# A message-passing layer on one core: edge tiles of 121 edges in blocks of 24, gathered into a ring of 192 tiles

## Chip, cores and metric

The kernel runs on one core of one Trainium2 chip. The metric is the device time in microseconds (us) of one execution; lower is better. All arithmetic is float32.

## What is computed

There are 12,500 nodes with 128 features, and 400,000 edges, each with a source, a destination and 64 attributes. The destinations are sorted. Cut to what matters:

```python
h = maximum(layernorm(x), 0)
m = relu(concat([h[src], edge_attr]) @ msg_w1 + msg_b1) @ msg_w2 + msg_b2
agg = segment_sum(m, dst, num_segments=12500)
u = relu(concat([h, agg]) @ upd_w1 + upd_b1)
out = x + u @ upd_w2 + upd_b2
```

## The kernel before, in words

**Node stage.** 25 groups of 500 nodes (NP = 125 partitions by ROWS = 4). VectorE takes the row statistics, ScalarE normalises, TensorE turns each group and multiplies it with the source part of the message weights. The product plus bias, `table`, is a 12,500 by 128 array in DRAM, stored by `store_table` on SP's queue (L295). TensorE also forms `update`, the node part of the update layer, which stays in SBUF transposed. Meanwhile GpSimd (POOL) gathers raw rows of `x` for the first 75 edge tiles (`early`, L368), because the table doesn't exist yet.

**Edge stage.** 3,200 tiles of EDGES = 125 edges, five tiles (TILES) to a chunk, so 640 chunks. One gather is one indirect DMA on POOL's queue: it fetches 125 rows of 512 bytes into one tile, one row in each partition (L380). Before its five gathers a chunk waits for its indices (L281 loads them on SP's queue after VectorE is done with the chunk that had the slot). The ring `rows` holds five chunks, 25 tiles. Per chunk:

- TensorE multiplies the attributes with their weights (L433, five matmuls with 64 rows of contraction, 128 columns each), one chunk ahead;
- VectorE adds the gathered rows into `hidden` (`sum_rows`, L785), ScalarE applies the relu (L613);
- VectorE builds a 0/1 mask of 5 by WINDOW = 128 columns (`make_masks`, L826), which says which node of a window of 128 nodes each edge goes to, and adds the five masks up (`sum_masks`, L834);
- TensorE sums the hidden rows of the chunk by node (`hidden_sums`, L467, five matmuls into one PSUM region), VectorE copies this out (`copy_sums`, L841), TensorE multiplies it with the joined weights (`update_sums`, L476, L477), and VectorE adds the result to 128 columns of `update` at the chunk's base (`accumulate`, L849).

The first 15 chunks used are the "early" ones (EARLY = 15): their rows are normalised, turned and multiplied on the spot (L443 to L454), one of them among ten others in each of the 15 rounds of the first loop. The engines have fixed orders of work, written out in loops over five slots; semaphores tie them together. A branch (`dve.If(span < WINDOW)`) takes a slow path if any chunk spans 128 nodes or more.

**Final stage.** When all edges are added, ScalarE takes the relu of `update` (L649), TensorE multiplies by the last weights (L542), VectorE adds to `x_all` (L946), which has stayed in SBUF since the start with the bias added during the edge stage (L910), and SP stores it (L343).

## Time and profile before

| | |
|---|---|
| median of 3 runs | 4913.87 us (4913.0 to 4914.27) |
| the profiled execution | 4917.07 us |
| its span in the trace | 4915.3 us |
| mean granted TensorE clock, of full speed | 0.608 |
| busy: PE, DVE, ACT, POOL | 71%, 46%, 12%, 79% |
| gathers | 75 of `x`, 3,125 of `table` |

The span runs from the first to the last recorded instruction. "Busy" of POOL's gather is the time that the record of the instruction covers; "idle before" is the gap ahead of it, and "issue" means that the gap waited for nothing that the profile shows. A queue's name ends in q (SPq). Rows of the trace are quoted in a section of their own below.

### The profile page before, as it was taken

The page shows a single profiled execution, that of the slowest core. Times are in us where ns is not written, and L with a number is a line of the kernel's source. Part 1 is how long each engine was busy: PE and PEld are TensorE (multiplying, and loading weights), DVE is VectorE, ACT ScalarE, POOL GpSimd, SP SyncE. Part 2 cuts the span into 40 slices and gives each one's busy share as a digit, 9 for nine tenths or more (in the row PEclk, how much of TensorE's full clock was granted, in tenths as well). Part 3 has the DMA queues.
Part 4 walks back from the last instruction along what each step waited for, and adds up shares of the span by engine and source line. Part 5 has one row for each costly group of instructions (what it writes and reads, how often), then busy time and mean ns, then how long its engine had stood idle before and what let it go on. Part 6 is the DMA issues. An engine that isn't in the chain of part 4 may idle for free.

```text
span 4915.3 us, 59369 instructions
## 1 busy us (share of the span) xinstructions
PE 3511.1 (71%) x16139; PEld 3183.0 (65%) x16139; DVE 2248.7 (46%) x3651; ACT 595.7 (12%) x887; POOL 3881.7 (79%) x3208
## 2 busy tenths in 40 slices
PE   5677777777677767766777677767776677767766
PEld 3666666666666666666666666666666666666666
DVE  5455555555444444444444444444444444444444
ACT  5111111111100000001010001000100010001002
POOL 7777777777778787877777777777777777777774
PEclk8666666666655555556555655655565655565566
DMA  7322222222222222222222222222222222222223
GB/s 174 73 67 64 69 66 67 68 66 67 64 64 64 65 65 64 64 64 64 64 66 64 64 64 65 64 64 64 65 65 64 64 64 66 64 64 64 65 64 87
DMA packets 398534, 336.04 MB, mean 68 GB/s; under 512 B 287275, under 2 KB 304299, under 8 KB 397263
## 3 DMA queue, kind: packets, MB, share of 16 engines
q0 software_dynamic: 256000, 208.52, 18.0%
q1 hardware_dynamic: 141810, 126.99, 10.5%
q10 hardware_dynamic: 706, 0.33, 0.0%
q8 instruction: 6, 0.10, 0.0%
q14 instruction: 12, 0.10, 0.0%
HBM read 319.26 MB, written 12.81 MB: 68 GB/s over the span
## 4 chain that ended last, share of the span: by engine, by line
POOL 72%; issue 23%; PE 2%; SPq 1%; DMA 1%; POOLq 0%; DVE 0%; another core or an unknown queue 0%; ACT 0%; ACTq 0%; DVEq 0%
POOL rows L380 72%; SPq L281 1%; PE pre L542 0%; POOLq L374 0%; PE seg L403 0%; DMA rows<-table,index 0%; PE pre L407 0%; PE pre L395 0%; POOLq L378 0%; DMA table<-space 0%; PE seg L467 0%; DMA b_upd_col<-in_b_upd 0%; DVE space L716 0%; PE iota_ps L542 0%
## 5 line engine op out<-in xcount | busy, mean ns | idle before, releaser
L380 POOL DMA_INDIRECT rows<-table,index x3125 | 3789.7, 1213 | 953.9 <-issue 953.0
L467 PE MATMUL seg<-space,hidden 125*128 125x128 f32 x6400 | 1517.1, 420 | 1030.1 <-ACT hidden L613 697.5
L467 PEld LDWEIGHTS seg<-space,hidden 125*128 125x128 f32 x6400 | 1353.0, 316 | 1166.2 <-issue 640.8
L785 DVE TENSOR_TENSOR hidden<-pre,rows 125x640 f32<-125x640 f32 x625 | 514.9, 824 | 1826.4 <-DMA rows<-table,index 1614.0
L433 PE MATMUL pre<-w_attr_sb,attr_space 64*125 64x128 f32 x6250 | 1304.0, 384 | 15.1 <-issue 15.1
L433 PEld LDWEIGHTS pre<-w_attr_sb,attr_space 64*125 64x125 f32 x6250 | 1173.1, 284 | 116.1 <-issue 103.7
L613 ACT ACTIVATE hidden<-hidden 125x640 f32<-125x640 f32 x640 | 471.5, 737 | 4247.4 <-DVE hidden L785 3476.0
L834 DVE TENSOR_REDUCE part_space<-space 125x128 f32<-125x640 f32 x640 | 790.6, 1235 | 0.0
L826 DVE TENSOR_TENSOR space<-iota_ps,dst_rel 125x640 f32<-125x640 f32 x640 | 526.0, 822 | 118.3 <-DVE part_space L834 71.1
L476 PE MATMUL seg<-part_space,w_msg_t_sb 128*128 128x128 f32 x1280 | 393.4, 407 | 224.8 <-DVE part_space L834 208.4
L476 PEld LDWEIGHTS seg<-part_space,w_msg_t_sb 128*128 128x128 f32 x1280 | 319.8, 306 | 258.7 <-issue 258.5
L477 PE MATMUL seg<-part_space,b_msg_rep 125*128 125x128 f32 x1280 | 371.4, 389 | 0.0
L849 DVE TENSOR_TENSOR update<-seg,update 128x128 f32 x640 | 186.6, 292 | 301.1 <-PE seg L477 151.9
L477 PEld LDWEIGHTS seg<-part_space,b_msg_rep 125*128 125x128 f32 x1280 | 319.9, 306 | 0.0
L841 DVE COPY part_space<-seg 128x128 f32<-128x128 f32 x640 | 181.3, 283 | 259.1 <-PE seg L467 166.6
L368 POOL DMA_INDIRECT early<-in_x,index_early x75 | 91.0, 1213 | 31.6 <-issue 27.8
L443 PE MATMUL pre<-w_attr_sb,attr_space 64*125 64x128 f32 x150 | 51.2, 436 | 20.6 <-issue 20.6
L454 PE MATMUL pre<-identity,space 125*128 125x125 f32 x75 | 19.5, 425 | 50.0 <-ACT space L626 43.1
L443 PEld LDWEIGHTS pre<-w_attr_sb,attr_space 64*125 64x125 f32 x150 | 31.9, 265 | 35.5 <-issue 33.3
L445 PE MATMUL pre<-w_src_sb,space 128*125 128x128 f32 x150 | 53.5, 455 | 0.0
L454 PEld LDWEIGHTS pre<-identity,space 125*128 125x128 f32 x75 | 13.7, 219 | 53.5 <-issue 53.5
L395 PEld LDWEIGHTS pre<-identity,rows 125*128 125x128 f32 x100 | 12.7, 160 | 53.2 <-issue 39.0
(65 smaller groups left out, 503.9 us busy)
## 6 DMA issues: line engine op xcount, KB each, us to landing
attr_space<-in_attr SPq DMA_DIRECT2D x640, 156.2 KB
rows<-table,index POOLq DMA_INDIRECT x3125
index<-in_src SPq DMA_DIRECT2D x625, 2.4 KB
table<-space SPq DMA_DIRECT2D x25, 224.0 KB
out<-x_all SPq DMA_DIRECT2D x4, 1120.0 KB
x_all<-in_x SPq DMA_DIRECT2D x2, 1120.0 KB
x_all<-in_x SPq DMA_DIRECT2D x1, 2240.0 KB
attr_space<-in_dst_rows SPq DMA_DIRECT2D x2, 781.2 KB
```

Of the source, the lines that this page charges most:

```text
L368: pool.indirect_dma_start(early[:, c, t, :], None, x, bass.IndirectOffsetOnAxis(index_early[:, c, t:t + 1], 0))\
L380: pool.indirect_dma_start(rows[0:EDGES, k, t, :], None, table, bass.IndirectOffsetOnAxis(index[:, k, t:t + 1], 0))\
L433: last = pe.matmul(pre[0:EDGES, k % 2, t * D:(t + 1) * D], attrs[:, k, t * EDGES:(t + 1) * EDGES], w_attr_sb[0:K_ATTR, :], start=True, sto ...
L467: last = pe.matmul(seg[:, 0, 0:WINDOW], hidden[0:EDGES, hidden_slot(k), t * D:(t + 1) * D], mask[:, k % 2, t, :], start=(t == 0), stop=(t ...
L476: pe.matmul(seg[:, 1, 0:WINDOW], w_both[:, :], part[:, k % 2, :], start=True, stop=False)
L477: pe.matmul(seg[:, 1, 0:WINDOW], bias_both[0:EDGES, :], mask_sum, start=False, stop=True).then_inc(seg_ready, 1)
L613: act.activation(hidden[0:EDGES, slot, :], hidden[0:EDGES, slot, :], ACT.Relu).then_inc(relued, 1)
L785: dve.tensor_tensor(hidden[0:EDGES, k, :], pre[0:EDGES, k % 2, 0:TILES * D], rows[0:EDGES, k].rearrange("p t d -> p (t d)"), ALU.add).then ...
L826: dve.tensor_tensor(mask[:, k % 2], iota[0:EDGES, 0:WINDOW].unsqueeze(1).to_broadcast([EDGES, TILES, WINDOW]), dst_rel[:, bass.ds(c, 1), : ...
L834: dve.tensor_reduce(mask_sum, mask[:, k % 2].rearrange("p t w -> p w t"), AX_X, ALU.add)\
L841: dve.tensor_copy(part[:, k % 2, :], seg[:, 0, 0:WINDOW]).then_inc(part_copied, 1)
L849: dve.tensor_tensor(columns, seg[:, 1, 0:WINDOW], columns, ALU.add).then_inc(accumulated, 1)
```

## The change

- **Tiles.** EDGES goes from 125 to 121. 400,000 edges fill 3,306 tiles, the last one padded (26 edges more). Each tile is still one gather on POOL (L391 of the new kernel). The diff sets no number of DMA engines; the change's name says 11 for a gather of 121 rows.
- **Blocks.** A block is 24 tiles: three "pairs" (PAIRS = 3) of 8 tiles (PAIR = 8). There are 137 whole blocks and one of 18 tiles. Masks, their sums and the copy are made per block; the relu and the sum with the gathered rows per 8 tiles, in place in the ring.
- **Window.** 80 nodes for each 8 tiles in place of 128 for 5; `update` is added to in three instructions a block. The branch to the slow path is now at a span of 80.
- **Attributes.** Two tiles are stacked in the 128 partitions (the attributes' 64 rows twice), and `w_attr_sb` becomes block-diagonal, 128 by 256: one matmul gives the products of two tiles.
- **Ring.** SLOTS = 8 blocks, 192 tiles: `rows` has four, and the space of `x_all` the other four. A block's gathers wait until TensorE's `hidden_sums` of the block 8 before is done. Indices are loaded 5 blocks ahead (AHEAD).
- **Early tiles.** 3 blocks, 72 gathers of `x`, done as the first blocks. Table gathers: 3,234.
- **Node stage.** Groups are 500 consecutive nodes. The bases of the windows come from a DRAM round trip of the tiles' first destinations, ahead of the last five table stores on SP's queue.
- **Final stage.** `x_all` is overwritten, so ScalarE loads `x` again (`load_x`). Since the destinations are sorted, 23 of the 25 groups are finished between blocks 120 and 134 (FINISH), and two after the last block. A second condition of the branch checks that no later window reaches back into a finished group.

The core of the diff:

```diff
-EDGES = 125
-TILES = 5
-WINDOW = 128
-EARLY = 15
+EDGES = 121
+PAIR = 8
+PAIRS = 3
+TILES_B = PAIRS * PAIR
+SLOTS = 8
+AHEAD = 5
+WINDOW = 80
+EARLY = 3
...
-        rows = sb("rows", [P, UNROLL, TILES, D])
+        rows = sb("rows", [P, SLOTS // 2, TILES_B, D])
+        rows_late = x_all[:, 0:SLOTS // 2 * TILES_B * D].rearrange("p (s t d) -> p s t d", s=SLOTS // 2, t=TILES_B)
+        attrs = sb("attrs", [2 * K_ATTR, 2, PAIRS * COLUMNS])
...
+            sp.wait_ge(firsts_made, UNROLL)
+            sp.dma_start(firsts[0].rearrange("(p t) -> p t", t=DT), firsts_sb[:, :]).then_inc(firsts_stored, 16)
+            sp.dma_start(dst_sb, dst_cols).then_inc(cols_loaded, 16)
+            sp.wait_ge(firsts_stored, 16)
+            sp.dma_start(first_bc, firsts[:, 0:ALL_TILES].to_broadcast([P, ALL_TILES])).then_inc(firsts_loaded, 16)
+            store_table(GBODIES - 1)
...
-            with pool.Fori(0, BODIES) as i:
-                for k in range(UNROLL):
-
-                    pool.wait_ge(index_loaded[k], i * 16 + 16)
-                    pool.sem_inc(pool_turns, 1)
-                    for t in range(TILES):
-                        pool.indirect_dma_start(rows[0:EDGES, k, t, :], None, table,
-                                                bass.IndirectOffsetOnAxis(index[:, k, t:t + 1], 0))\
-                            .then_inc(gathered[k], 16)
+            def gather(source, j, tiles):
+                for t in range(tiles):
+                    pool.indirect_dma_start(slot_rows(j)[:, t, :], None, source, bass.IndirectOffsetOnAxis(index[0:EDGES, j, t:t + 1], 0))\
+                        .then_inc(gathered[j][t // PAIR], 16)
+
+            def gather_block(i, j):
+                b = block_of(i, j)
...
+                    pool.wait_ge(index_loaded[j], i * 16)
+                need(pool, hidden_summed, b - (SLOTS - 1))
+                pool.sem_inc(pool_turns, 1)
+                gather(table, j, TILES_LAST if isinstance(b, int) and b == LAST else TILES_B)
...
-                    last = pe.matmul(pre[0:EDGES, k % 2, t * D:(t + 1) * D], attrs[:, k, t * EDGES:(t + 1) * EDGES],
-                                     w_attr_sb[0:K_ATTR, :], start=True, stop=True)
+                return pe.matmul(columns(j, q, PAIR)[:, two * 2 * D:(two + 1) * 2 * D], attrs[:, j % 2, start:start + EDGES],
+                                 w_attr_sb[:, :], start=True, stop=stop)
```

**Order on POOL.** The two rows are the edge loop's body before, after the 75 gathers of `x`:

```order
L368 DMA early<-in_x,index_early 125x128 x75
...
L380 DMA rows<-table,index 125x128 x25
L374 REGISTER_ALU
L374 COMPARE_AND_BRANCH
```

In the change the same place on POOL reads as follows, up to the start of the loop and its end (`x_all` is the other half of the ring):

```order
L391 DMA rows<-in_x,index 121x128 x72
L391 DMA rows<-table,index 121x128 x24
L391 DMA x_all<-table,index 121x128 x96
...
L391 DMA x_all<-table,index 121x128 x48
L413 REGISTER_ALU
L413 COMPARE_AND_BRANCH
L391 DMA rows<-table,index 121x128 x96
```

The queue holds gathers and nothing else, as before; each now has 121 partitions.

**Order on PE.** One step of the edge stage before, in the first loop (the steps of the second loop are the same; `space` holds the mask):

```order
L433 MATMUL pre<-w_attr_sb,attr_space 125x128 [waits summed]
L433 MATMUL pre<-w_attr_sb,attr_space 125x128 x4
L463 REGISTER_ALU
L467 MATMUL seg<-space,hidden 128x128 [waits part_copied,relued,masks_made]
L467 MATMUL seg<-space,hidden 128x128 x4
L476 MATMUL seg<-part_space,w_msg_t_sb 128x128 [waits accumulated,mask_sums_made,part_copied]
L477 MATMUL seg<-part_space,b_msg_rep 128x128
```

One block of the change, in its first round (`h_space` holds the copied sums):

```order
L467 MATMUL pre<-w_attr_sb,attrs 121x256 [waits summed]
L467 MATMUL pre<-w_attr_sb,attrs 121x256 x3
L529 MATMUL spare<-h_space,w_msg_t_sb 128x240 [waits accumulated,mask_sums_made,part_copied]
L530 MATMUL spare<-h_space,b_msg_rep 128x240
L513 MATMUL seg<-space,rows 128x80 [waits part_copied,relued,masks_made]
L513 MATMUL seg<-space,rows 128x80 x7
L467 MATMUL pre<-w_attr_sb,attrs 121x256 [waits summed,attr_loaded0]
L467 MATMUL pre<-w_attr_sb,attrs 121x256 x3
L513 MATMUL seg<-space,rows 128x80 [waits relued]
L513 MATMUL seg<-space,rows 128x80 x7
```

Four attribute matmuls of 256 columns now stand for eight tiles, the sums by node are 80 columns wide, and the two update matmuls come once for 24 tiles.

## Rows read from the trace of the kernel before

**Rows 1.** The page: busy time, share of the span and instructions of each engine.

```profile
PE 3511.1 (71%) x16139; PEld 3183.0 (65%) x16139; DVE 2248.7 (46%) x3651; ACT 595.7 (12%) x887; POOL 3881.7 (79%) x3208
```

**Rows 2.** The page: the chain that ended last, by engine.

```profile
POOL 72%; issue 23%; PE 2%; SPq 1%; DMA 1%; POOLq 0%; DVE 0%; another core or an unknown queue 0%; ACT 0%; ACTq 0%; DVEq 0%
```

**Rows 3.** The page's groups, GpSimd gathers: busy, mean ns | idle before, releaser.

```profile
L380 POOL DMA_INDIRECT rows<-table,index x3125 | 3789.7, 1213 | 953.9 <-issue 953.0
...
L368 POOL DMA_INDIRECT early<-in_x,index_early x75 | 91.0, 1213 | 31.6 <-issue 27.8
```

**Rows 4.** Timeline of POOL from 2000 us: start, length, instruction, idle before it.

```profile
1999.38 1.21 POOL L380 DMA_INDIRECT rows<-table,index  x1 [0.30 <-issue]
2000.90 1.21 POOL L380 DMA_INDIRECT rows<-table,index  x1 [0.30 <-issue]
...
2029.68 1.21 POOL L380 DMA_INDIRECT rows<-table,index  x1 [0.30 <-issue]
```

**Rows 5.** One tile, rows: its gathers' shortest, median and longest.

```profile
L380 POOL DMA_INDIRECT rows<-table,index x3125: 1205/1210/4500, 126.1 to 4866.7; - x196
```

**Rows 6.** The page's DMA queues: packets, MB, share of 16 engines.

```profile
q0 software_dynamic: 256000, 208.52, 18.0%
```

**Rows 7.** Timeline, all engines, 116 to 150 us.

```profile
120.00 0.69 DVE L716 TENSOR_TENSOR space<-seg,b_msg_bc 125x512 f32<-125x512 f32 x1 [1.57 <-remote]
...
123.09 1.21 POOL L368 DMA_INDIRECT early<-in_x,index_early  x1 [0.30 <-issue]
126.08 1.21 POOL L380 DMA_INDIRECT rows<-table,index  x1 [1.78 <-issue]
...
132.09 3.47 DVE L774 TENSOR_TENSOR dst_rel<-dst_rel,base_bc 125x3200 f32<-125x3200 int32 x1
...
132.15 4.50 POOL L380 DMA_INDIRECT rows<-table,index  x1 [0.30 <-issue]
```

**Rows 8.** The chain of waits between 115 and 130 us.

```profile
121.42 3.48 DMA table<-space
```

**Rows 9.** Timeline from the last gather to the final stage.

```profile
4866.72 1.21 POOL L380 DMA_INDIRECT rows<-table,index  x1 [0.30 <-issue]
...
4870.17 0.82 DVE L785 TENSOR_TENSOR hidden<-pre,rows 125x640 f32<-125x640 f32 x1 [4.06 <-DMA rows<-table,index]
...
4878.36 0.29 DVE L849 TENSOR_TENSOR update<-seg,update 128x128 f32 x1 [1.44 <-PE seg L477]
4881.91 11.08 ACT L649 ACTIVATE hidden<-update 128x500 f32 x11 [10.14 <-DVEq L936]
```

**Rows 10.** SP's waits: engine line <- releaser: us in total, times, longest.

```profile
SPq L94 <- DMA out<-x_all: 2.8, 1, 2.8
```

**Rows 11.** The page's groups of the edge stage on PE, DVE and ACT.

```profile
L467 PE MATMUL seg<-space,hidden 125*128 125x128 f32 x6400 | 1517.1, 420 | 1030.1 <-ACT hidden L613 697.5
L467 PEld LDWEIGHTS seg<-space,hidden 125*128 125x128 f32 x6400 | 1353.0, 316 | 1166.2 <-issue 640.8
L785 DVE TENSOR_TENSOR hidden<-pre,rows 125x640 f32<-125x640 f32 x625 | 514.9, 824 | 1826.4 <-DMA rows<-table,index 1614.0
L433 PE MATMUL pre<-w_attr_sb,attr_space 64*125 64x128 f32 x6250 | 1304.0, 384 | 15.1 <-issue 15.1
...
L613 ACT ACTIVATE hidden<-hidden 125x640 f32<-125x640 f32 x640 | 471.5, 737 | 4247.4 <-DVE hidden L785 3476.0
L834 DVE TENSOR_REDUCE part_space<-space 125x128 f32<-125x640 f32 x640 | 790.6, 1235 | 0.0
L826 DVE TENSOR_TENSOR space<-iota_ps,dst_rel 125x640 f32<-125x640 f32 x640 | 526.0, 822 | 118.3 <-DVE part_space L834 71.1
L476 PE MATMUL seg<-part_space,w_msg_t_sb 128*128 128x128 f32 x1280 | 393.4, 407 | 224.8 <-DVE part_space L834 208.4
...
L477 PE MATMUL seg<-part_space,b_msg_rep 125*128 125x128 f32 x1280 | 371.4, 389 | 0.0
L849 DVE TENSOR_TENSOR update<-seg,update 128x128 f32 x640 | 186.6, 292 | 301.1 <-PE seg L477 151.9
...
L841 DVE COPY part_space<-seg 128x128 f32<-128x128 f32 x640 | 181.3, 283 | 259.1 <-PE seg L467 166.6
```

**Rows 12.** Busy time by stretch, 1400 to 2400 us, with granted clock.

```profile
1400.00:2400.00 1000.00, 713.42 (x3167) 652.67 (x3166) 443.55 (x677) 96.51 (x131) 799.60 (x658) 0.58 0.27 64
```

More of the change, by code:

```diff
@@ L30 @@
+import itertools
+import math
 from contextlib import ExitStack
@@ new lines, in load_block @@
+            def load_block(i, j):
+                b = block_of(i, j)
+                nxt = ahead(i, j, AHEAD)
+                if exists(*nxt) and not (isinstance(b, int) and b + AHEAD < SLOTS):
+                    need(sp, summed, b * PAIRS + (PAIRS - (SLOTS - AHEAD) * PAIRS))
+                    load_index(*nxt)
+                load_attr(i, j)
+            sp.wait_ge(update_ready, after(GROUPS - 1))
+            for j in range(SLOTS):
+                load_block(0, j)
+            with sp.Fori(1, ROUNDS) as i:
+                for j in range(SLOTS):
+                    load_block(i, j)
@@ L354, in _ @@
+            for i in range(ROUNDS, -(-(LAST + 1) // SLOTS)):
+                for j in rounds_of(i):
+                    load_block(i, j)
         @block.gpsimd
@@ new lines, in finish_group, with finish_groups @@
+            def finish_group(g):
+                pe.wait_ge(u_relued, g + 1)
+                need(pe, o_made, g)
+                for r in range(ROWS):
+                    last = pe.matmul(spare[0:NP, r * D:(r + 1) * D], u[:, r, :], w_upd2_sb[:, :], start=True, stop=True)
+                last.then_inc(o_ready, 1)
+            def finish_groups(i, j):
+                b = block_of(i, j)
+                for g, at in FINISH.items():
+                    if isinstance(b, int) and at == b:
+                        pe.wait_ge(accumulated, (b - 1) * PAIRS)
+                        finish_group(g)
@@ new lines, in copy_sums, with accumulate @@
+            def copy_sums(i, j):
+                if not exists(i, j):
+                    return
+                b = block_of(i, j)
+                width = pairs_of(b) * WINDOW
+                dve.wait_ge(hidden_summed, b + 1)
+                need(dve, seg_ready, b - 1)
+                dve.tensor_copy(part[:, j % 2, 0:width], seg[:, j % 2, 0:width]).then_inc(part_copied, 1)
+            sites = itertools.count()
+            def accumulate(i, j):
+                if not exists(i, j):
+                    return
+                b = block_of(i, j)
+                site = next(sites)
+                registers = [dve.alloc_register(f"base{c}_of_{site}") for c in range(pairs_of(b))]
+                dve.load(registers, base_row[0:1, bass.ds(b * BASES, pairs_of(b))])
+                for c in range(pairs_of(b)):
+                    base = bass.RuntimeValue.of_register_unchecked(registers[c], min_val=0, max_val=N - 1)
+                    if c == 0:
+                        dve.wait_ge(seg_ready, b + 1)
+                    need(dve, accumulated, b * PAIRS + c)
+                    place = update[:, bass.ds(base, WINDOW)]
+                    dve.tensor_tensor(place, spare[:, c * WINDOW:(c + 1) * WINDOW], place, ALU.add).then_inc(accumulated, 1)
@@ L869, in accumulate_wide @@
                     dve.wait_ge(wide_ready, m + 1)
[L870 to L871 removed]
+                    place = update[:, bass.ds(w * WIDE, WIDE)]
+                    dve.tensor_tensor(place, spare[:, 0:WIDE], place, ALU.add).then_inc(wide_added, 1)
                     dve.wait_ge(wide_added, m + 1)
[L875 to L896 removed]
@@ new lines, in edge_loops @@
+                one = divmod(LAST - 1, SLOTS)
+                two = divmod(LAST, SLOTS)
+                make_masks(*one)
+                for q in range(PAIRS):
+                    if q < PAIRS - 1:
+                        sum_rows(*one, q)
+                    if q == 0:
+                        sum_masks(*behind(*one, 1))
+                        copy_sums(*behind(*one, 1))
+                        accumulate(*behind(*one, 2))
+                    if q == 1:
+                        finish_groups(*one)
@@ new lines, in edge_loops @@
+                make_masks(*two)
+                sum_masks(*one)
+                sum_rows(*one, PAIRS - 1)
+                for q in range(PAIRS_LAST):
+                    sum_rows(*two, q)
+                accumulate(*behind(*one, 1))
+                copy_sums(*one)
+                sum_masks(*two)
+                copy_sums(*two)
+                accumulate(*one)
+                accumulate(*two)
+                dve.wait_ge(accumulated, LAST * PAIRS + PAIRS_LAST)
+                for g in REST:
+                    finish_group(g)
```

943 lines of the change are left out of this document (564 added, 379 removed).

## The prediction, made before any run of the changed kernel

> **What bounds the kernel now.** I read the page's busy times first. No engine is full: POOL 3,881.7 us of 4,915.3 (79%), PE 3,511.1 (71%), DVE 2,248.7 (46%) [rows 1]. The chain of waits then says which of them sets the end: 72% of it is POOL and 23% "issue" [rows 2], and both are the gathers, since 953.0 of POOL's 953.9 us of idle time ahead of them is "issue" [rows 3]. So POOL waits for nobody; the gap belongs to the gather. The timeline shows how regular it is: 1999.38 to 2029.68 holds 20 gathers, 30.30 / 20 = 1.515 us from start to start, of which 1.21 is recorded as busy and 0.30 is the gap [rows 4]. The shortest gather took 1.205 and the median 1.210 [rows 5], so data, DMA traffic and the other engines don't matter to it. PE, DVE and ACT wait for rows (DVE's `sum_rows` 1,614.0 us for gathers [rows 11]).
>
> The profiled execution adds up as: first table gather at 126.08 [rows 7]; 3,125 x 1.515 = 4,734; this gives 4,860, while the last gather began at 4866.72 [rows 9] and ended its period at 4868.2, so 8 us went to odd stalls; from there to the end 47 us. Sum 4,915.3, the span. The execution's own time was 4,917.1 and the median of the runs 4,913.9, 1.4 below the span. I forecast the span and take that difference as nothing. A measurement can tell about 0.2%, some 10 us, from no change.
>
> **The change, part by part.** The sum is start + gathers x period + stalls + tail.
>
> *Start.* POOL begins at about 5.5 us as before; its 72 gathers of `x` end by 5.5 + 72 x 1.515 = 115, sooner if they are cheaper. Then it waits for the table. Before, 75 gathers ended at 124.3 and the table's last store landed at 121.42 + 3.48 = 124.9 [rows 7, 8], so the two were even. In the change the table is the later one. Its last stores now stand on SP's queue behind a wait for a DRAM round trip and two loads of 1.6 MB, but the last groups are only made at 120.0 [rows 7], and the round trip can start one body of five groups earlier. I take 127 for the first table gather; bounds 120 (stores sooner) and 140 (stores behind the loads).
>
> *Count.* 3,306 - 72 = 3,234 table gathers in place of 3,125.
>
> *Period of a gather.* This term decides, and no row shows it for 121 rows, since all 3,200 gathers have 125. Three things could carry the 1.213 us of busy time; the 0.302 of the gap I leave. It may be the instruction itself (unchanged). It may be the rows (x 121/125 = 0.968). Or it may be what POOL has to write for the DMA engines. The DMA queue row bears on the last: 256,000 packets for 3,200 gathers is 80 each, 5 for each of 16 engines; 208.52 MB / 3,200 is 65,162 bytes where the rows are 125 x 512 = 64,000 [rows 6]. The 1,162 extra bytes fit 16 marks of 4 bytes plus 11 x 25 x 4 = 1,100: as if 5 engines carried 25 rows each and each of the 11 idle ones were given 25 dummy entries of 4 bytes. Then POOL writes 16 x 26 = 416 entries a gather, and with 11 rows on each of 11 engines 16 x 12 = 192, x 0.462.
>
> The Trainium skill, "DMA: Bandwidth & Descriptors", section on why a DMA increments its semaphore by 16, says that a DMA uses the largest number of engines up to 16 that divides its rows, and that a gather's completion is posted by all 16. By that rule 125 rows take 5 engines and 121 take 11; the byte count agrees with the 5.
>
> The ends are 1.515 (all of the busy time is the instruction) and 0.302 + 1.213 x 0.462 = 0.862 (all of it entries). Below that end nothing, above it a dearer engine share (a rival). With nothing in the rows to weigh the three, I give each a third: 1.213 x (1 + 0.968 + 0.462) / 3 = 0.982, plus 0.302 = **1.284 us**. 3,234 x 1.284 = 4,152.
>
> *Stalls.* 4 us. One gather took 4.50 in place of 1.21, exactly beside DVE's subtraction of the bases, 3.47 us with both operands in SBUF [rows 7]. The change has one such operation of the same length, of 3,304 columns. The Trainium skill, "SBUF — State Buffer", "SBUF: two separate sides", calls the port pair that VectorE and GpSimd share an exclusive lock, which an operation with two SBUF inputs takes; the row agrees. The new steady block has no such operation (each sum has an operand in PSUM), so the lock costs nothing more.
>
> *Tail.* Before: rows landed, and DVE added them, 3.45 us after the last gather began (4870.17), the last add to `update` was at 4878.36, the final stage began at 4881.91 and lasted to 4915.3, 33.4 us for 25 groups [rows 9]. Now only two groups are left. From the end of the last period: landing 2; DVE's queue of about 8 (a masks' sum for 18 tiles, 18/5 of 1.235 less the narrower window = 2.8 us; two copies of 0.5; nine adds of 0.3 with loads of the bases, 4); two groups of 4 us each (a relu of 1.1, a sum of 0.7, matmuls and handoffs); the store with its wait of 2.8 [rows 10] about 4. Together **22** us; bounds 15 and 35.
>
> *Work beside it, costed at nothing.* At a granted clock of 0.58 (the lower level, 1.2 GHz, most of the time [rows 12]) PE's busy time per tile was 1304.0/3125 = 0.417 for attributes and 1517.1/3200 = 0.474 for sums, and (393.4 + 371.4)/640 = 1.195 a chunk for the update [rows 11]. For 24 tiles: 12 products of twice the columns 10.0; sums 24 x 0.474 x 80/128 = 7.1, or 10.1 if the weight load (1353.0/3200) bounds it; update 2.2. That is 19 to 22 us, 0.81 to 0.93 per gather. DVE: mask 2.5, sums 4.0, masks' sum 3.7, copy 0.5, adds 0.9, 11.6 us or 0.48; ACT 3 x 1.2 = 3.5. POOL covers all of these as long as its period stays above 0.93. Its new wait (TensorE done with the block eight before) has seven blocks of lead, some 200 us. The early blocks are the place where it could show: nine steps of about 13 us from about 140 on end near 260, and POOL asks for the first of them only after 120 table gathers, at 127 + 154 = 281. The reload of `x`, the stores and the finishing of groups from block 120 on hold up ACT and DVE by some 10 us in a block of 31; nobody on the chain waits there. If POOL were faster than 0.93, PE would be late next.
>
> *Sum:* 127 + 4,152 + 4 + 22 = **4,305 us**, 12.4% below 4,915. In general 153 + 3,234 x period; the change pays from a period below (4,915 - 153)/3,234 = 1.473.
>
> **The rivals.**
>
> *A, the price is per gather (slower).* The period stays at 1.515: 153 + 4,900 = 5,053 us. For it: the spread of 1.205 to 1.210 looks like a fixed program. Against it: the dummy bytes. It decides above 1.473, that is if less than 0.042 us of the 1.515 goes away. The same page of the Trainium skill, under where the 2 us go, calls descriptor generation small and says that many can be emitted before it shows. By that rule the extra 106 gathers are simply paid. The trace so far speaks half against it: 1.2 us of POOL per gather isn't small. Chance 18%.
>
> *B, the price is per row.* Busy time x 0.968 gives 1.476 and 4,926 us; the gap scaled too gives 1.466 and 4,896. The row count is then the same (400,026 for 400,000) and only the shorter tail pays. Chance 8%, of which 3 faster by over 0.2% and 5 within it.
>
> *C, each engine that carries rows costs POOL more (slower).* If a fifth of the busy time is for five engines, 0.049 each, 11 cost 0.29 more and the period is near 1.8: about 5,970 us. For it: nothing but that 11 is more than 5. Chance 7%.
>
> *D, nearly all is entries, and PE becomes the bound.* 153 + 3,234 x 0.862 = 2,941 if POOL holds, 3,306 x 0.93 + 150 = 3,225 if PE does. Chance 7%.
>
> *E, the change doesn't do what it says:* a window of 80 is overrun and the slow path runs, or the early blocks stall POOL. The densest destinations (400,000 / (2 x 12,500) = 16 edges a node at the end of the square law) put 968 edges on about 61 nodes, well under 80. Chance 2%, slower.
>
> **The numbers.** The forecast's own case, a period from 1.08 to 1.46, has 58%: its low end is two thirds of the busy time by entries, 1.213 x (1 - 0.667 x 0.538) + 0.302 = 1.08, so 153 + 3,497 = 3,650. The range goes on up through B and A to 5,053 with a table 12 us later, 5,065. Left out: D (7%) and C and E (9%). Faster by over 0.2%: 58 + 7 + 3 = 68%; within: 5%; slower: 18 + 7 + 2 = 27%.
>
> **What would show it.** The gathers' mean and gap in the page's groups: busy near 0.98, gap near 0.30; 1.21 means A, 1.17 B, 1.5 C, 0.56 D. The software queue's packets: still 80 a gather, but only 121 x 512 + 64 + 5 x 11 x 4 = 62,236 bytes, so 205.8 MB; any other sum breaks the dummy entries. POOL should stay on most of the chain, with waits for TensorE near nothing; the first table gather near 127; the last stretch after POOL's end near 22 us. The forecast is wrong if POOL's idle time names PE or an index load, or if the period doesn't follow the entries at all.

## The result, and the profile after

The changed kernel took 5,141.57 us (median of 4 runs, 5,121.51 to 5,196.03) against 4,914.07 for the kernel before: a ratio of 1.0481, 95% interval 1.0397 to 1.0565, so slower by 5%. The forecast was 4,305, and its range ended at 5,065: both missed. The profiled execution took 5,128.71 us, its span is 5,127.0.

The page of the changed kernel: busy times; the chain, by engine and by line; the groups of gathers and of TensorE's attribute products and sums; the software queue.

```profile
PE 2567.1 (50%) x11242; PEld 2089.2 (41%) x11242; DVE 1520.5 (30%) x1660; ACT 561.7 (11%) x652; POOL 3383.8 (66%) x3314
...
PE 47%; issue 46%; another core or an unknown queue 2%; DVE 2%; ACT 1%; ACTq 0%; DMA 0%; DVEq 0%; SPq 0%
PE seg L513 22%; PE pre L467 21%; PE spare L529 1%; PE spare L530 1%; PE spare L563 1%; DVE space L999 1%; DMA space<-firsts 0%; ACT h_space L684 0%; ACT rows L734 0%; ACT h_space L773 0%; DVE rows L959 0%; DVE stats_early L966 0%; DVE rows L953 0%; ACT rows L722 0%
...
L391 POOL DMA_INDIRECT rows<-table,index x1602 | 1640.3, 1024 | 829.5 <-issue 588.5
L391 POOL DMA_INDIRECT x_all<-table,index x1632 | 1668.7, 1022 | 764.5 <-issue 596.0
L467 PE MATMUL pre<-w_attr_sb,attrs 128*121 128x256 f32 x3306 | 1178.5, 486 | 419.4 <-issue 354.0
L513 PE MATMUL seg<-space,rows 121*128 121x80 f32 x3348 | 616.1, 303 | 935.4 <-issue 922.6
...
q0 software_dynamic: 158688, 205.75, 15.6%
```

The gathers got cheaper, 1.02 us busy where it was 1.21 [rows 3]. But POOL is busy for 66% only (79% in [rows 1]) and has left the chain, of which it was 72% [rows 2]: now it is TensorE, and "issue". TensorE is busy for 50% and idle for "issue" ahead of its own matmuls, that is, it waits for nothing the profile shows. The timeline of POOL says who stops the gathers:

```profile
2018.21 1.02 POOL L391 DMA_INDIRECT x_all<-table,index  x1 [0.31 <-issue]
2024.52 1.02 POOL L391 DMA_INDIRECT x_all<-table,index  x1 [5.28 <-PE seg L513]
2025.85 1.02 POOL L391 DMA_INDIRECT x_all<-table,index  x1 [0.31 <-issue]
```

Between stops the period is 1.327 us (2024.52 to 2025.85). The stop is the wait for `hidden_summed`: the ring is full, TensorE is eight blocks behind. The timeline of TensorE shows how it came to that. Each line is a run of matmuls, with their number at its end (the trace has two records for each fp32 product):

```profile
1963.86 1.91 PE L513 MATMUL seg<-space,x_all 121*128 121x80 f32 x16
1965.60 1.93 PE L467 MATMUL pre<-w_attr_sb,attrs 128*121 128x256 f32 x8
...
1979.92 0.29 PE L513 MATMUL seg<-space,x_all 121*128 121x80 f32 x1 [1.80 <-issue]
1981.32 0.29 PE L513 MATMUL seg<-space,x_all 121*128 121x80 f32 x1 [1.10 <-issue]
1982.02 0.50 PE L513 MATMUL seg<-space,x_all 121*128 121x80 f32 x1 [0.41 <-issue]
...
2022.64 0.29 PE L513 MATMUL seg<-space,x_all 121*128 121x80 f32 x1 [1.80 <-issue]
2023.34 0.29 PE L513 MATMUL seg<-space,x_all 121*128 121x80 f32 x1 [0.41 <-issue]
...
2028.39 1.91 PE L513 MATMUL seg<-space,x_all 121*128 121x80 f32 x16
```

Sixteen records take 1.91 us at 1963.86, and again at 2028.39. Between them the same records come one by one, 0.70 us apart or a multiple of it (1981.32 to 1982.02, 1979.92 to 1981.32). The busy time of the same stretch, in three pieces (PE busy and its number of records, PEld, DVE, ACT, POOL, granted clock, DMA share, GB/s):

```profile
1960.00:1972.00 12.00, 12.00 (x69) 10.79 (x68) 5.85 (x4) 2.11 (x2) 9.26 (x10) 0.86 0.21 54
1972.00:2023.00 51.00, 13.20 (x38) 9.49 (x37) 5.12 (x7) 2.11 (x2) 36.57 (x36) 0.55 0.22 60
2023.00:2032.00 9.00, 8.66 (x39) 7.37 (x38) 7.82 (x8) 2.11 (x2) 5.95 (x6) 0.71 0.26 65
```

69 records in 12 us, then 38 in 51 us, then 39 in 9. A clock at its lower level (0.5, 1.2 GHz) would double the time of a record; it doesn't put 1.3 us between them. I call such a stretch a **hold-up**. Counted from the trace (weight loads of one line that start 0.6 to 4.5 us apart), they hold 2,830 us of the changed kernel's span and 4 us of the kernel's before.

Two more places. The first is the start. POOL's timeline, the last early gather and the first of the table; then TensorE's timeline in the node stage:

```profile
97.61 1.02 POOL L391 DMA_INDIRECT rows<-in_x,index  x1 [0.31 <-issue]
177.09 3.91 POOL L391 DMA_INDIRECT rows<-table,index  x1 [78.46 <-issue]
```

```profile
25.93 1.00 PE L442 MATMUL pre<-attrs,w_node_sb 128*128 128x500 f32 x2
46.63 1.10 PE L430 MATMUL pre<-identity,h_space 125*128 125x125 f32 x4 [19.69 <-issue]
55.78 2.07 PE L438 MATMUL seg<-w_src_sb,attrs 128*125 128x128 f32 x8 [8.05 <-DVE attrs L856]
...
95.08 1.07 PE L430 MATMUL pre<-identity,h_space 125*128 125x125 f32 x4 [35.87 <-DVE attrs L856]
```

While POOL gathers from `x` (to 98.6) the node stage all but stands, and it goes on once POOL is done. TensorE has 14 records from 30 to 90 us and 265 from 100 to 160:

```profile
30.00:90.00 60.00, 4.52 (x14) 2.91 (x14) 3.20 (x9) 5.38 (x11) 46.28 (x46) 0.54 0.39 89
100.00:160.00 60.00, 46.65 (x265) 31.82 (x266) 42.54 (x118) 50.26 (x99) 0.00 (x0) 0.91 0.41 118
```

The same stretch of the same kernel with 125 edges a tile (5 queues; experiment 8), where POOL gathers from `x` just as long:

```profile
30.00:90.00 60.00, 43.49 (x233) 28.73 (x231) 39.03 (x115) 42.80 (x86) 47.84 (x40) 0.91 0.70 182
```

So the table comes at 177.1, not at 126.1 [rows 7]. The second is the end: the last gather begins at 5000.61 and the kernel ends at 5,127.0, as TensorE still has a full ring to work off.

```profile
5000.61 1.02 POOL L391 DMA_INDIRECT rows<-table,index  x1 [0.30 <-issue]
```

### The profile page after: what moved, and what is told of

It is laid out like the page before. It is cut to its first block, busy times and chain, and to the rows that moved or that the text cites. A ratio compares the mean times of both kernels' runs of the same rounds, so it can differ in the third digit from the quotient of the medians.

```text
span 5127.0 us, 33848 instructions
## 1 busy us (share of the span) xinstructions
PE 2567.1 (50%) x11242; PEld 2089.2 (41%) x11242; DVE 1520.5 (30%) x1660; ACT 561.7 (11%) x652; POOL 3383.8 (66%) x3314
## 3 DMA queue, kind: packets, MB, share of 16 engines
q0 software_dynamic: 158688, 205.75, 15.6%
## 4 chain that ended last, share of the span: by engine, by line
PE 47%; issue 46%; another core or an unknown queue 2%; DVE 2%; ACT 1%; ACTq 0%; DMA 0%; DVEq 0%; SPq 0%
PE seg L513 22%; PE pre L467 21%; PE spare L529 1%; PE spare L530 1%; PE spare L563 1%; DVE space L999 1%; DMA space<-firsts 0%; ACT h_space L684 0%; ACT rows L734 0%; ACT h_space L773 0%; DVE rows L959 0%; DVE stats_early L966 0%; DVE rows L953 0%; ACT rows L722 0%
## 5 line engine op out<-in xcount | busy, mean ns | idle before, releaser
L391 POOL DMA_INDIRECT rows<-table,index x1602 | 1640.3, 1024 | 829.5 <-issue 588.5
L391 POOL DMA_INDIRECT x_all<-table,index x1632 | 1668.7, 1022 | 764.5 <-issue 596.0
L467 PE MATMUL pre<-w_attr_sb,attrs 128*121 128x256 f32 x3306 | 1178.5, 486 | 419.4 <-issue 354.0
L513 PE MATMUL seg<-space,rows 121*128 121x80 f32 x3348 | 616.1, 303 | 935.4 <-issue 922.6
L513 PE MATMUL seg<-space,x_all 121*128 121x80 f32 x3264 | 582.4, 300 | 893.9 <-issue 892.9
L467 PEld LDWEIGHTS pre<-w_attr_sb,attrs 128*121 128x121 f32 x3306 | 730.1, 233 | 731.5 <-issue 573.5
L513 PEld LDWEIGHTS seg<-space,rows 121*128 121x128 f32 x3348 | 577.6, 230 | 994.5 <-issue 970.3
L513 PEld LDWEIGHTS seg<-space,x_all 121*128 121x128 f32 x3264 | 556.6, 228 | 928.9 <-issue 915.4
L1013 DVE TENSOR_REDUCE h_space<-space 121x240 f32<-121x1920 f32 x138 | 466.1, 3378 | 0.0
L999 DVE TENSOR_TENSOR space<-iota_ps,dst_rel 121x1920 f32<-121x1920 f32 x138 | 297.0, 2152 | 5.8 <-issue 5.8
L391 POOL DMA_INDIRECT rows<-in_x,index x72 | 73.7, 1024 | 23.2 <-issue 21.7
```

Source lines behind the costliest of these rows:

```text
L391: pool.indirect_dma_start(slot_rows(j)[:, t, :], None, source, bass.IndirectOffsetOnAxis(index[0:EDGES, j, t:t + 1], 0))\
L467: return pe.matmul(columns(j, q, PAIR)[:, two * 2 * D:(two + 1) * 2 * D], attrs[:, j % 2, start:start + EDGES], w_attr_sb[:, :], start=Tru ...
L513: last = pe.matmul(seg[:, j % 2, q * WINDOW:(q + 1) * WINDOW], slot_rows(j)[:, q * PAIR + t, :], mask[:, j % 2, q, t, :], start=(t == 0), ...
L999: dve.tensor_tensor(mask[:, j % 2].rearrange("p c t w -> p (c t) w")[:, 0:tiles, :], iota[0:EDGES, 0:WINDOW].unsqueeze(1).to_broadcast([ED ...
L1013: last = dve.tensor_reduce(mask_sum[:, j % 2, 0:pairs * WINDOW].rearrange("p (c w) -> p c w", c=pairs), mask[:, j % 2, 0:pairs].rearrange( ...
```

## The experiments

**1. What a gather costs, and whether dense matmuls alone are slow.** Two kernels with nothing of the reference in them. The first issues 14 sections of 50 gathers, each section with another number of rows:

```python
for t in range(N_G):
    pool.indirect_dma_start(*one(128, t)).then_inc(landed[t], 16)
```

> Sections of 50 gathers, each with its own row count, nothing waiting. Leaves the reference out. Entries theory (busy time of a gather is a fixed part plus 0.0136 us for each ring entry, fixed by the two rows of the traces, 1.213 at 125 rows on 5 queues and 1.023 at 121 on 11): 128 rows 0.98 us busy, 126 rows 1.00, 120 rows 0.98, 112 rows 0.96, 64 rows 0.93, a gap of 0.30 after each. Rival (rows theory, the third of the forecast: 0.0032 us a row): 64 rows 0.2 us below 128. Rival (each queue costs): 128 rows on 16 queues dearer than 121 on 11, about 1.2 us.

The groups of the gathers, here those of 127, 124, 119, 121, 120 and 128 rows:

```profile
L46 POOL DMA_INDIRECT rows<-in_x,index x50 | 127.5, 2550 | 17.7 <-issue 17.7
L52 POOL DMA_INDIRECT rows<-in_x,index x50 | 64.5, 1290 | 17.7 <-issue 17.7
...
L61 POOL DMA_INDIRECT rows<-in_x,index x50 | 55.0, 1101 | 17.8 <-issue 17.5 <-DMA rows<-in_x,index 0.3
L55 POOL DMA_INDIRECT rows<-in_x,index x50 | 51.1, 1022 | 18.2 <-issue 13.4 <-DMA rows<-in_x,index 4.7
...
L58 POOL DMA_INDIRECT rows<-in_x,index x50 | 49.1, 982 | 17.5 <-issue 12.8 <-DMA rows<-in_x,index 4.7
...
L43 POOL DMA_INDIRECT rows<-in_x,index x50 | 47.2, 944 | 17.9 <-issue 14.0 <-DMA rows<-in_x,index 3.9
```

125 rows took 1.213 us, 64 rows 0.907 and 16 rows 0.958. The Trainium skill, "DMA: Bandwidth & Descriptors", section on why a DMA increments its semaphore by 16, gives the queues by the largest divisor of the rows up to 16: 1, 4, 7, 11, 15 and 16 for those above. The packets of the traces bear it out: a gather of 121 rows leaves 22 packets that carry rows (4,096 and 1,536 bytes, 11 of each) and 10 of 32 and 12 bytes (5 of each), which are 11 queues with 11 rows and 5 with 11 dummy entries of 4 bytes. The time follows the queues too. Counting as entries those of one queue, which are its rows and one more, 125 rows (26 entries) to 127 (128 entries) is (2.550 - 1.213) / 102 = 0.0131 us an entry, and from 125 on it gives 1.29 for 124 rows (measured 1.290), 1.11 for 119 (1.101), 1.03 for 121 (1.022) and 0.99 for 120 (0.982). Over 16 queues the line is less good: it gives 0.99 for 128 rows (0.944) and 0.90 for 16 rows (0.958). Rows show no price of their own: 64 and 128, both over 16 queues, differ by 0.037, less than the 4 entries between them would give (0.052). No dearer queue shows either: 16 of them are the cheapest.

The second kernel loops over dense matmuls on TensorE, of both kernels' shapes and mixes, with pauses between its sections:

```python
section(6, 60, lambda: (attr2(attrs, both, 0, 4), sums(rows, 121, mask, 80, 8))[1])
```

> TensorE alone, in loops of 8 to 16 matmuls with nothing to wait for, 11 sections of 100 to 400 us apart by about 50 us of idling: the attribute products on zero and on dense weights, with 64 and with 128 rows, the sums of 80 and of 128 columns, and the mixes of both kernels. Leaves the reference out. Limiter theory (a long dense stretch at 2.4 GHz sets off intervals of 0.70 us a matmul): most sections show such intervals, within 20 us of the clock's rise; a section of zeros shows fewer if the data matter. Instruction theory (the large loop body can't be fetched in time): none in any section, as each loop holds 16 matmuls at most. Attribute theory (it is the full 128-row, 256-column product): only in the sections that hold it.

No section was slow, on chip 3 and not even in 200 us at the full clock, so the theory of a limiter that dense work alone sets off falls. Busy time by stretch (attribute products, sums of 80 columns, the changed kernel's mix):

```profile
400.00:500.00 100.00, 100.00 (x466) 85.23 (x465) 0.00 (x0) 0.00 (x0) 1.00 0.00 0
1100.00:1200.00 100.00, 100.00 (x471) 100.00 (x470) 0.00 (x0) 0.00 (x0) 0.50 0.00 0
2450.00:2550.00 100.00, 100.00 (x683) 92.82 (x682) 0.00 (x0) 0.00 (x0) 1.00 0.00 0
```

**2. The kernel before with more queues.** One constant each (and the last chunk filled up for 126):

```diff
-EDGES = 125
+EDGES = 128
```

> The kernel before with 128 edges a tile, 3,125 gathers over 16 queues. Period theory with the period that the entries give (0.98 busy + 0.30): 150 + 3,125 x 1.28 = 4,150 us, TensorE (0.82 us a gather) below it, no matmul intervals of 0.70 us, since TensorE still works in bursts of five tiles and waits between them. Rival (each queue costs): 1.5 us a gather, 4,850 us. Rival (any kernel whose TensorE comes near its bound is slowed to 0.70 us a matmul): above 4,600 us with TensorE named by the idle time of the gathers.

> The kernel before with 126 edges a tile, 3,175 gathers over 14 queues, 10 entries each. Period theory: 1.00 busy + 0.30 gap, 150 + 3,175 x 1.30 = 4,275 us, above the kernel of 128 edges by 3%. Rival (each queue costs): 1.45 us a gather, 4,750 us. Rival (TensorE slowed): above 4,600 us.

With 128 edges 5,630 us (ratio 1.1451, 1.1432 to 1.1470), with 126 edges 5,840 us (1.1878, 1.1822 to 1.1934): the last rival of both expectations. The gathers were as cheap as the first experiment says, 944 ns, and POOL stood idle for nearly as long as it worked:

```profile
L380 POOL DMA_INDIRECT rows<-table,index x3050 | 2880.6, 944 | 2595.0 <-DMA index<-in_src 1534.8
```

The index loads wait on SP's queue for `summed`, and that for TensorE, whose records have gaps of 10 to 20 us. They don't look like the hold-ups above: the count that gave 2,830 us there gives 6 us here, as TensorE does its bursts at pace and then stands still. That both are one thing is argued from what brings them on, the rows of a gather and the chip (experiment 7), and not shown record by record. Still, nothing in the changed kernel's new structure is needed for a loss, and its large loop body isn't either. What these kernels share with it is gathers over more than 5 queues.

**3. TensorE's mix beside one other engine's work at a time**, and the two halves of the change apart. The mix kernel loops over 4 attribute products and 8 sums while POOL, SP, VectorE or ScalarE do theirs:

```python
PLAN = [(0, 0, 0, 0), (125, 0, 0, 0), (121, 0, 0, 0), (128, 0, 0, 0), (0, 1, 0, 0), (0, 0, 1, 0), (0, 0, 0, 1),
        (125, 1, 1, 1), (121, 1, 1, 1), (128, 1, 1, 1)]
```

> TensorE runs the changed kernel's mix of products (4 attribute products of 128 rows by 256 columns, 8 sums of 80 columns) with nothing to wait for, alone and beside one other engine's work at a time: gathers of 125, 121 and 128 rows, loads by SP, sums by VectorE, activations by ScalarE, and all of them. Leaves the reference out. Alone a turn of 12 products takes 3.5 us at 2.4 GHz. Contention theory (gathers that go over many queues hold TensorE up): turns of over 8 us in the sections of 121 and 128 rows and none in that of 125. Theory of a limiter of the whole core: slow turns only where all engines work, whatever the gathers. Theory that only TensorE's waits bring it out: no slow turn anywhere.

The halves: the changed kernel with `EDGES = 125` (5 queues), and the kernel before with `EDGES = 121` (11 queues).

> The changed kernel with 125 edges a tile: everything as there, but 3,200 gathers of 125 rows over 5 queues. Contention theory (the slow intervals of TensorE come with gathers over many queues): no interval of 0.70 us a matmul, gathers at 1.515 us, 150 + 3,200 x 1.515 = 5,000 us plus an end of 60 us. Theory that dense bursts of blocks of 24 tiles bring it out: the slow intervals stay, above 5,150 us.

> The kernel before with 121 edges a tile and its chunks of 5 tiles, 3,200 gathers over 11 queues; the last 12,800 edges are left out. Contention theory: TensorE is held up as with 126 and 128 edges, above 5,200 us. Theory that it needs 14 or 16 queues in this structure: period 1.327, 150 + 3,200 x 1.327 = 4,400 us.

The mix kernel: no section slow, 1,822 us. The changed kernel with 125 edges: 4,892 us. The kernel before with 121 edges (and without the last 12,800): 4,302 us, nothing held up, the period 1.327. By this the contention theory looked dead, and the slow runs of experiment 2 stood against it. I took the length of TensorE's loop body for the difference next.

**4. Long bodies, chains of waits, and slower gathers.** The mix again, unrolled 6 or 30 times, in some sections chained to VectorE and ScalarE by semaphores; and three kernels with a register load ahead of gathers to slow them:

```diff
                 for t in range(tiles):
+                    if t % 2:
+                        pool.load([idle], index[0:1, j, t:t + 1])
                     pool.indirect_dma_start(slot_rows(j)[:, t, :], None, source, bass.IndirectOffsetOnAxis(index[0:EDGES, j, t:t + 1], 0))\
```

> Leaves the reference out. TensorE's mix again, now in long bodies (30 mixes of 12 products in a row, or 6) and in some sections in a chain with VectorE and ScalarE, so that it waits on semaphores; alone and beside gathers of 125, 121 and 128 rows. Instruction theory (a long body's instructions can't be fetched while gathers go over many queues): the sections of 30 mixes beside 121 and 128 rows hold intervals of 0.70 us a matmul, those of 125 rows or none don't. Theory of the waits (they come only where TensorE waits on semaphores beside such gathers): only in the chained sections with 121 or 128 rows. Theory of a mere rate (TensorE fed faster than it can take): nowhere.

> The changed kernel with a register load on GpSimd ahead of every second gather, which does nothing but take time: period of about 1.5 us in place of 1.327, the 11 queues as they are. Theory of the queues (gathers over many queues hold TensorE up): intervals of 0.70 us a matmul as before, above 5,150 us. Theory of the rate (the intervals come when TensorE is fed so fast that it works long at 2.4 GHz): they go, and the time is 180 + 3,234 x 1.5 + 50 = 5,080 us or, if the load takes less, the period times 3,234 plus 230.

> The kernel of 128 edges with such a load ahead of four gathers in five: period about 1.5 us with 16 queues. Theory of the queues: TensorE held up as without it, about 5,600 us. Theory of the rate: 150 + 3,050 x 1.5 + 75 x 1.5 = 4,840 us, faster than the same kernel without the loads.

> The same with the load ahead of two gathers in five: period about 1.37 us. Theory of the queues: 5,600 us. Theory of the rate: between, 4,440 us if 1.37 us is slow enough (the kernel of 121 rows with the chunks of before ran at 1.34 without being held up).

The register loads were a miss: the period stayed at 1.327 and 1.25 us, and the times stayed too (5,132, 5,648, 5,617 us). They say nothing on the rate, which stays untested. In the mix kernel all sections beside 121 and 128 rows were slow, chained or not, and none beside 125 rows or none. With 6 mixes in the body as with 30. It looked like the body's length, but one thing had changed beside it: the chip.

**5. The number of queues, and the body's length.** 18 sections, body, turns, rows of a gather, loads by SP:

```python
PLAN = [(6, 6, 125, 0), (6, 6, 114, 0), (6, 6, 119, 0), (6, 6, 81, 0), (6, 6, 100, 0), (6, 6, 121, 0), (6, 6, 108, 0),
        (6, 6, 117, 0), (6, 6, 120, 0), (6, 6, 64, 0), (6, 6, 16, 0), (6, 6, 0, 1),
        (1, 41, 128, 0), (2, 20, 128, 0), (3, 13, 128, 0), (4, 10, 128, 0), (5, 8, 128, 0), (4, 10, 121, 0)]
```

> Leaves the reference out. TensorE alone with its mix of 12 products, no waits, 18 sections. Twelve have a body of 6 mixes (72 products) beside gathers of 125, 114, 119, 81, 100, 121, 108, 117, 120, 64 and 16 rows (5, 6, 7, 9, 10, 11, 12, 13, 15, 16 and 16 queues) and beside 24 loads of 0.7 MB by SP; six have bodies of 1, 2, 3, 4 and 5 mixes beside gathers of 128 rows and of 4 mixes beside 121. Theory of the queues: full pace (67 to 70 records in 10 us) up to some number of queues between 5 and 11 and 3 to 5 records from there on, whatever the rows; with 16 rows on 16 queues as slow as with 64. Theory of the bytes or entries in flight: 16 rows at full pace. Theory of instruction supply: bodies of 1 or 2 mixes at full pace, longer ones slow; loads by SP at full pace if it is GpSimd's way of issuing that takes the room, slow if any traffic does.

Busy time in stretches of 20 us; the number that counts is PE's (x...). In order: gathers of 125 rows (5 queues), 114 (6), 119 (7), 81 (9), 121 (11), 16 rows (16 queues), no gathers but loads by SP, and 128 rows beside a body of one mix. (The columns are PE, PEld, DVE, POOL, clock, DMA share, GB/s.)

```profile
110.00:130.00 20.00, 20.00 (x140) 18.60 (x139) 0.00 (x0) 15.83 (x14) 1.00 0.18 43
300.00:320.00 20.00, 15.93 (x66) 13.02 (x66) 0.00 (x0) 15.73 (x15) 0.73 0.17 41
560.00:580.00 20.00, 11.01 (x25) 6.43 (x25) 0.00 (x0) 15.73 (x15) 0.50 0.18 45
830.00:850.00 20.00, 3.79 (x7) 1.96 (x7) 0.00 (x0) 15.20 (x16) 0.50 0.13 32
1430.00:1450.00 20.00, 2.04 (x7) 2.02 (x8) 0.00 (x0) 15.43 (x16) 0.50 0.19 47
2925.00:2945.00 20.00, 2.03 (x7) 2.20 (x8) 0.00 (x0) 14.67 (x18) 0.50 0.03 7
3165.00:3185.00 20.00, 20.00 (x140) 18.63 (x140) 0.00 (x0) 0.00 (x0) 1.00 0.81 257
3420.00:3440.00 20.00, 2.03 (x7) 2.01 (x7) 0.00 (x0) 15.12 (x17) 0.50 0.20 53
```

The hold-up follows the queues, by degrees: 140 records with 5, 66 with 6, 25 with 7, 7 or 8 from 9 on. It isn't the bytes: SP's loads move 257 GB/s and cost TensorE nothing, gathers of 16 rows move 7 GB/s and hold it up in full. It isn't a large number of entries: 16 rows make the fewest. And it isn't the body's length: one mix is as slow as six.

One rival is left, though. In all these sections more queues also mean fewer entries in each (26 with 125 rows, 20 with 114, 18 with 119, 12 or fewer from 9 queues on) and gathers in quicker succession (one in 1.515, 1.43, 1.41 and 1.33 us or less). No run has many queues and slow gathers, or 5 queues and quick ones, as gathers of 5 or 25 rows would be. Against the mere rate speaks that the kernel with 128 edges lost its 15% with a gather every 1.80 us on the mean (5,635.7 / 3,125). So "over many queues" names the gathers that hold TensorE up; that it is the number of queues that does it isn't shown.

The hold-up also comes and goes late. In the sections of mixes it begins 9 to 18 us after the first gather (9 and more queues), and it outlasts the last packets of the gathers, which come 2 to 3 us after the last gather's begin: TensorE is back at full pace 12 us after that begin with 121 rows, 19 to 24 with 128 and 29 with 16. So it isn't the transfers in flight as such that hold it up.

**6. The whole kernel before with 121 edges**, 665 chunks, 10 early chunks:

```diff
-EDGES = 125
+EDGES = 121
-EARLY = 15
+EARLY = 10
-        bounds = sb("bounds", [CP, 3, UNROLL])
+        bounds = sb("bounds", [CP, 3, SHARE])
```

> The kernel before with 121 edges a tile, whole: 665 chunks of 5 tiles (the last 2,325 edges are filled up), 10 early chunks in place of 15, 7 shares of the destinations a partition in place of 5. Period theory, as the kernel that left 12,800 edges out bore out: 120 + 3,275 x 1.328 + 40 = 4,510 us, nothing of TensorE held up. Rival (with 11 queues the hold-up comes by chance, and the shorter kernel was lucky): above 4,700 us, or rounds that differ by over 1%.

6,050 us, ratio 1.2316 (1.2296 to 1.2337), where its shorter twin had taken 4,302: the rival of the expectation, but its five runs agree within 0.6%, so not by chance from run to run. The results of the experiments name the chip they ran on (the changed kernel's own four runs in the first section name none). The twin, the mix kernel and the changed kernel with 125 edges had run on chip 7, and every experiment that was slow on chips 3, 6 and 2.

**7. The same kernels on another chip**, word for word:

> The kernel before with 121 edges a tile and the last 12,800 edges left out, once more, word for word. It ran in 4,302 us with nothing held up, while the whole kernel with 121 edges ran in 6,050 us. Theory that the chip decides (the run of 4,302 us was on another chip than those that were held up): on this chip about 5,800 us. Theory that the program decides: 4,302 us again.

> The first kernel of TensorE's mix beside other engines' work, once more, word for word (leaves the reference out). On the chip before no section was slow. Theory that the chip decides: the sections beside gathers of 121 and 128 rows fall to 4 records in 10 us, and the kernel takes about 2,300 us in place of 1,822. Theory that the program decides: 1,822 us again.

> The changed kernel once more, word for word, beside them. Theory that the chip decides: about 5,140 us where the other two are slow, and about 180 + 3,234 x 1.327 + 50 = 4,500 us where they are fast. Theory that the program decides: 5,140 us whatever the other two do.

On chip 3 they took 5,789, 2,278 and 5,165 us: the twin up from 4,302, the mix up from 1,822, each within 1% of what the theory of the chip gave. The kernel before took 4,914 and 4,924 us on the two chips, so the difference is in what the gathers of 121 rows do. Each of these is one run. The same stretch of the mix kernel, beside gathers of 121 rows, on chip 7:

```profile
490.00:510.00 20.00, 20.00 (x141) 18.67 (x140) 0.00 (x0) 0.00 (x0) 15.43 (x16) 1.00 0.18 47
```

and on chip 3, with the same gathers at the same pace:

```profile
490.00:510.00 20.00, 2.62 (x7) 2.27 (x8) 0.00 (x0) 0.00 (x0) 15.43 (x16) 0.50 0.19 47
```

**8. The changed kernel with few queues.** `EDGES = 125`, five runs, and `EDGES = 119` (7 queues), one; both on chip 1.

> The changed kernel with 125 edges a tile, word for word the one that took 4,892 us, now against the kernel before in five rounds. Theory of the queues (5 queues never hold TensorE up, on any chip): 4,892 us, 0.4% under the kernel before, whatever the chip, which makes it faster than both. Rival (it was fast for its chip alone): above 5,100 us on a chip of the other kind.

> The changed kernel with 119 edges a tile: 3,362 gathers of 119 rows over 7 queues, 1.10 us busy and 0.30 gap. In TensorE's mix alone 7 queues left it 13 records in 10 us, against 4 with 11. Theory of the queues, by degrees: GpSimd's floor is 180 + 3,290 x 1.40 = 4,790 us; stretches of 0.70 us a record are rarer or shorter than with 11 queues, and the time lies between this floor and 5,140 us. If this chip is of the kind that holds nothing up, 4,790 to 4,850 us.

With 125 edges 4,890.36 us (4,888.08 to 4,898.65) against 4,911.87, ratio 0.9956 (0.9942 to 0.9969): 0.4% under the kernel before, and 5% under the changed kernel's 5,142 (not run on this chip). With 119 edges 4,990.55 us, between its floor and 5,140, with 2,469 us of hold-ups by the count above. That chip 1 is of the common kind the second shows: its gathers run at their price, and TensorE is idle for "issue" as in the changed kernel, if for less.

```profile
L391 POOL DMA_INDIRECT rows<-table,index x1656 | 1828.0, 1104 | 615.0 <-issue 613.5 <-remote 1.5
...
L513 PE MATMUL seg<-space,rows 119*128 119x80 f32 x3456 | 719.4, 318 | 679.6 <-issue 672.3 <-ACT rows L722 4.0
```

In the kernel with 125 edges these sums have no idle time ahead of them; TensorE's waiting is ahead of the attribute products, and for VectorE's sums, which wait for rows:

```profile
L467 PE MATMUL pre<-w_attr_sb,attrs 128*125 128x256 f32 x3200 | 1452.0, 630 | 2166.9 <-DVE rows L959 1101.1 <-DVE x_all L959 1062.7 <-DVE h_space L990 3.1
...
L513 PE MATMUL seg<-space,rows 125*128 125x80 f32 x3264 | 464.3, 305 | 0.0
```

## Why the prediction was wrong

Against the forecast's four terms, in the profiled execution:

| term | forecast | measured | more |
|---|---|---|---|
| start | 127 | 177.1 | 50 |
| 3,234 periods | 1.284 each | 1.327 each | 139 |
| stalls | 4 | 5,001.9 - 177.1 - 4,291.5 = 533 | 529 |
| tail | 22 | 5,127.0 - 5,001.9 = 125 | 103 |

(5,001.9 is the last gather's begin and one period.) Together 821 us, 4,305 to 5,126.

**The step that failed is "Work beside it, costed at nothing".** Its sentence was "POOL covers all of these as long as its period stays above 0.93". TensorE's need was sized right: in the kernel with 125 edges it is busy for 2578.6 / 3,200 = 0.81 us a gather, the low end of the 0.81 to 0.93. What failed is that this need stays what it is beside other gathers. With 11 queues TensorE falls to 38 records in 51 us; a tile of the changed kernel needs (3,306 + 6,612 + 552) / 3,306 = 3.2 of them (products, sums, update), so 4.3 us for a tile that POOL brings every 1.327. A ring of "seven blocks of lead" then only puts off the stop. The step looked for cover in time (who is late) and not for what the covering work does to the covered one. It carries 529 of the 821, and the start and the tail with it, 682 in all.

**Start and tail** failed by that same cause. Where TensorE isn't held up they were right. The changed kernel with 125 edges, first and last gather of the table, on chip 7:

```profile
120.00 1.58 POOL L391 DMA_INDIRECT rows<-table,index  x1 [7.23 <-issue]
...
4867.88 1.21 POOL L391 DMA_INDIRECT x_all<-table,index  x1 [0.30 <-issue]
```

On chip 7 the start is 120.0 (bounds 120 to 140), the tail 4,890.4 - 4,869.4 = 21.0 (forecast 22), the stalls 10. The formula "153 + 3,234 x period" gives for its 3,128 gathers 153 + 3,128 x 1.515 = 4,892, and it took 4,892. On chip 1 the same kernel starts at 128.2 and has a tail of 19.4. With 119 edges, on chip 1 too, the start is 170.2: the loss at the start comes with the gathers' rows. So the block structure, the attribute products, the ring, the reload of `x` and the short final stage did what the prediction said of them, and are worth 0.4% by themselves.

**The period** had the right mechanism and a size off by 3%: busy 1.02 for 0.982. The thirds were wrong one by one. Rows carry nothing, entries 26 x 0.0131 = 0.34 of the 1.213 (a third is 0.40), the instruction 0.87. The queue's bytes came out as said (205.75 MB for 205.8), so the dummy entries are real; its packets didn't, 158,688 / 3,306 = 48 a gather for "still 80", since one packet takes up to 8 entries (4,096 bytes of rows or 32 of dummies). The point from which the change pays, 1.473, was passed by far: rivals A, B and C (per gather, per row, per queue) are all refuted, the gather alone even more cleanly by the first experiment. Two small slips of the sum change nothing: the low end, at a period of 1.08, is 3,646 for 3,650, and B's first time 4,927 for 4,926.

**The rivals** held none that ends slower because TensorE slows. E had "the early blocks stall POOL" at 2%; POOL was stopped, but 80 times for 2 us or more after the start, and for another cause. The text named the sign for it, "if POOL's idle time names PE", and gave it no price. A number for it was to be had: the work beside the gathers was costed from rows in which gathers use 5 queues, and the change moved them to 11. That was the same kind of unknown as the period and had deserved a range.

**What a faster version would be** here: of the widths tried in the changed kernel (119, 121, 125), only the one over 5 queues beat the kernel before. On chip 7 the changed kernel should take 120 + 3,234 x 1.327 + 10 + 21 = 4,443 us, an estimate from the terms above; it wasn't run there. The structure does help where TensorE is held up: on chip 3, 5,165 us against 5,789 for the kernel before with the same rows and 12,800 edges fewer.

**Open.** Why gathers over many queues hold TensorE up, on which path, whether the number of queues, the entries in each or the pace does it, and whether chip 7 differs in kind or in state (it was used for one set of runs only). What starts a hold-up wasn't isolated: in the changed kernel it begins on the median 10 us after the granted clock has gone to 1.0 in a dense stretch (1963 to 1972 above). What ends it is clearer: of 78 stretches of over 15 us, 69 end while POOL stands still, on the median 3.6 us into the pause, as at 2019.2 to 2023.3 above. So here it mostly feeds on itself: TensorE is late until the full ring stops POOL, and the stop lets it go. It can end otherwise: with 119 edges 25 of 51 such stretches end while POOL gathers.

## What to carry to other kernels

Price what runs beside a changed transfer again, not just the transfer: here 0.19 us saved on each gather cost TensorE up to 95% of its pace (7 records for 140). Before spreading gathers over more queues, put the kernel's matmuls beside such gathers in a loop and count records in 20 us; it is one run. And repeat a run that refutes a theory on a second chip before building on it.

## What the runs showed of the hardware that was not expected

- On chip 2 TensorE gets 140 records in 20 us beside gathers over 5 queues, 66 over 6, 25 over 7 and 7 or 8 over 9 to 16; chips 3 and 6 gave the same 7 beside 11 and 16; on chip 7 it gets 141 beside 11. On chip 1 only whole kernels ran, one of them held up. In a hold-up records start 0.70 us apart or a multiple of it, whatever their columns (80 or 256).
- The gathers leave VectorE alone (80 sums, one every 1.131 us whatever runs beside them, on chips 7 and 3) and ScalarE nearly so (an activation every 0.947 us, every 1.089 beside gathers of 128 rows and all else on chip 3).
- A hold-up outlives its gathers: their last packets come 2 to 3 us after the last gather's begin, TensorE's full pace 12 us (121 rows) to 29 us (16 rows) after it.
- A gather's busy time is within 0.06 us of 0.87 us and 0.0131 us for each entry of one queue. One row fewer can cost more than twice the time: 127 rows take 2.550, 128 take 0.944.
- The granted clock stood at 0.50 for sums of 80 columns that kept TensorE busy without a gap (x471 in 100 us, experiment 1) and at 1.00 for the mix that holds the same sums.
